# A fused cross-attention and gated feed-forward kernel: Q projected straight into transposed form, rotated over partition halves, and weights loaded in place

## The reference

```python
q = (layernorm(x) @ Wq).reshape(b, t, 32, 128)          # 32 query heads
k = (ctx @ Wk).reshape(b, t, 8, 128); v = (ctx @ Wv).reshape(b, t, 8, 128)
q, k = rope(q), rope(k)                                  # x*cos + rotate_half(x)*sin
logits = 30 * tanh(q.k * 0.0884 / 30)                    # 4 query heads share one k, v
w = softmax(where(mask, logits, -1e30))
x = x + tanh(g_xattn) * ((w @ v).reshape(b, t, 4096) @ Wo)
h = layernorm(x)
gate, up = h @ Wg, h @ Wu                                # 512 -> 1376, 4-bit weights
x = x + tanh(g_ffn) * float16((gate * sigmoid(gate) * up) @ Wd)
```

## Time and profile before

| | |
|---|---|
| median of 3 runs | 811.78 us (811.74 to 812.43) |
| the profiled execution | 811.05 us, span 809.3 us, mean granted clock 0.982 |
| busy in the span | PE 772.4, PEld 644.7, DVE 616.4, ACT 352.7, POOL 494.1 us |
| instructions | 12403 |

### The profile page before, as it was taken

The page is one execution under the profiler, slowest core; times in us unless marked ns, Lnnn a source line. Parts: engine busy times, 40 slices in busy tenths (PEclk is TensorE's granted clock), DMA queues, the critical chain, the costliest instruction groups (busy, mean ns, idle before and its releaser), DMA issues.

```text
span 809.3 us, 12403 instructions
## 1 busy us (share of the span) xinstructions
PE 772.4 (95%) x3905; PEld 644.7 (80%) x3905; DVE 616.4 (76%) x1290; ACT 352.7 (44%) x715; POOL 494.1 (61%) x391
## 2 busy tenths in 40 slices
PE   4799999999999999999999999999998689999998
PEld 3677888888888888888888888888876468888786
DVE  6798887788878887788878887786897587787531
ACT  3545443444345443444444443444443345555520
POOL 3689766566656666566665666567885466666400
PEclk9989999999999999999999999999999799999999
DMA  8410402010210201020111102020010134342011
GB/s 294 130 53 1 131 1 79 1 53 0 80 52 1 79 1 53 1 79 1 53 38 41 53 2 62 18 47 1 21 42 1 42 72 114 98 107 49 0 66 39
DMA packets 56995, 41.61 MB, mean 51 GB/s; under 512 B 22922, under 2 KB 44298, under 8 KB 56938
## 3 DMA queue, kind: packets, MB, share of 16 engines
q1 hardware_dynamic: 56938, 40.90, 17.3%
HBM read 38.77 MB, written 2.11 MB: 51 GB/s over the span
## 4 chain that ended last, share of the span: by engine, by line
PE 89%; DVE 6%; POOL 3%; issue 2%; ACT 1%; DMA 0%; DVEq 0%; ACTq 0%; POOLq 0%
PE ps_o L53 7%; PE ps_o L55 7%; PE ps_o L54 7%; PE bank_q L55 7%; PE bank_q L53 7%; PE bank_q L54 7%; PE ps_qT L1131 4%; PE bank_kv L54 3%; PE bank_kv L55 3%; PE bank_kv L53 3%; PE ps_pv L53 3%; PE ps_s L54 3%; PE ps_s L53 3%; PE ps_s L55 3%; PE ps_pv L54 2%; PE ps_pv L55 2%
## 5 line engine op out<-in xcount | busy, mean ns | idle before, releaser
L511 POOL TENSOR_TENSOR aT_lo<-attn,aT_hi 128x512 fp32r<-128x512 f32 x64 | 96.8, 1512 | 157.8 <-ACT aT_hi L679 157.8
L53 PE MATMUL bank_q<-wq_hi,xT_hi 128*128 128x512 f32 x256 | 108.4, 424 | 1.6 <-DVE wq_lo L807 1.6
L638 ACT CAST qT_hi<-ps_qT 128x512 fp32r<-128x512 f32 x64 | 37.5, 586 | 162.1 <-PE bank_kv L1132 88.7
L55 PE MATMUL bank_q<-wq_hi,xT_lo 128*128 128x512 f32 x256 | 102.8, 401 | 0.0
L54 PE MATMUL bank_q<-wq_lo,xT_hi 128*128 128x512 f32 x256 | 102.7, 401 | 0.0
L53 PE MATMUL ps_o<-wo_hi,aT_hi 128*128 128x512 f32 x256 | 101.0, 394 | 1.2 <-POOL acc L490 0.7
L54 PE MATMUL ps_o<-wo_lo,aT_hi 128*128 128x512 f32 x256 | 100.1, 391 | 0.0
L55 PE MATMUL ps_o<-wo_hi,aT_lo 128*128 128x512 f32 x256 | 100.1, 391 | 0.0
L524 POOL TENSOR_TENSOR roped<-q_cos,q_sin 128x512 f32<-128x512 f32 x61 | 79.1, 1296 | 12.2 <-DVE q_sin L833 12.2
L496 POOL TENSOR_TENSOR probs<-probs,keepT 128x512 f32<-128x512 f32 x64 | 83.7, 1308 | 3.0 <-ACT probs L655 2.9
L988 DVE SCALAR_TENSOR_TENSOR acc<-ps_o,tgates,acc 128x512 f32<-128x512 f32 x54 | 40.5, 751 | 54.5 <-PE ps_o L55 54.5
(11 more groups left out here) (220 smaller groups left out, 2218.1 us busy)
## 6 DMA issues: line engine op xcount, KB each, us to landing
wo_raw<-in_Wo SPq DMA_DIRECT2D x8, 1024.0 KB, 5.3
wq_raw<-in_Wq SPq DMA_DIRECT2D x7, 1024.0 KB, 5.8
packed<-in_gate_q SPq DMA_DIRECT2D x40, 64.0 KB, 2.2
packed<-in_up_q SPq DMA_DIRECT2D x40, 64.0 KB, 2.3
packed<-in_down_q SPq DMA_DIRECT2D x10, 256.0 KB, 3.3
acc<-in_x SPq DMA_DIRECT2D x8, 256.0 KB, 8.4
cT_raw<-in_ctx SPq DMA_DIRECT2D x8, 256.0 KB, 8.5
wkv_raw<-in_Wk SPq DMA_DIRECT2D x8, 256.0 KB, 5.9
```

Of the source, the lines that this page charges most:

```text
L53: nc.tensor.matmul(out, w_hi, m_hi, start=first, stop=False)
L55: return nc.tensor.matmul(out, w_lo, m_hi, start=False, stop=last)
L511: nc.gpsimd.tensor_tensor(aT_lo[:], attn[:], aT_hi[:].bitcast(F32), ALU.subtract).then_inc(a_split, 1)
L638: nc.scalar.copy(qT_hi[:], ps_qT[:])
```

## The change

- **Q is made transposed.** Job n makes, for one head and four sequences, the tile of 128 head columns by 512 tokens: 128 columns of Wq are at rest and the four sequences of x move (`make_q`). It writes to two banks in turn. Eight jobs make a group, in the order half, head; job s+4 runs in slot s, and the first four ahead of slot 0, for which four sequences must be ready (eight for job 4). Slots 60 to 63 have no job.
- **Q's transposes are gone**; K's stays (`transpose_k`).
- **The rotation** now lies across partitions. VectorE makes the cosine product over 128 partitions and the sine products over the partition halves, 64 by 512 each, reading one half of the bank and writing the other half of `q_sin` (`cos_q`). GpSimd adds into `q_rot`, an SBUF tile for both halves of the sequences. ScalarE and VectorE split Q from `q_rot`, not from a PSUM bank. A transposed table of cosine and sine comes in as another input, and rows of the mask's table are turned on TensorE once.
- **Weights in place.** The raw weights land where their `lo` part will stand, so that there are two raw buffers; a load waits for the projections that used the tile two groups before (q_done, kv_done, o_done). Wk and Wv are split in two parts of two blocks each (128x512), no longer in four of 128x256.
- **The start**: x of all sequences is normalised, turned and split ahead of slot 0, with VectorE subtracting for x and GpSimd for the first weights. The context follows beside slots 0 to 5.
- **No loop** over slots: all 67 are straight code. Some tiles of the feed-forward part lie elsewhere.

TensorE at a slot's start, before: four Q transposes, K's, then the old projection (the numbers tell the buffers apart).

```diff
-        wq_raw = sb("wq_raw", [P, KT, GC], F32)
...
+        def split_pair(name, shape, starts, hi, lo, raw):
+            starts.append(at[0])
+            par = len(hi)
+            hi.append(sb(f"{name}_hi{par}", shape, F32R))
+            raw.append(over(f"{name}_raw{par}", shape, F32, at[0]))
+            lo.append(sb(f"{name}_lo{par}", shape, F32R))
...
+        q_rot = sb("q_rot", [P, 2, HG, HALF, T], F32)
+        k_rot = sb("k_rot", [P, D], F32)
...
+        q_banks = [bank[:].rearrange("p (b t) -> p b t", b=HALF) for bank in (bank_q, bank_q2)]
...
+        def q_job(n):
+            return n // B, n % B // HALF, n % HALF
         def all_slots(eng, slot):
...
+            for s in range(SLOTS + 3):
+                slot(s)
...
+                def load_wq(g):
+                    wait(sp, q_done, (g - 1) * B)
+                    sp.dma_start(wq_raw[g % 2][:], wq_v[:, :, g * GC:(g + 1) * GC]).then_inc(ld_wq[g % 2], 16)
...
+                def rope(n):
+                    g, half, h = q_job(n)
+                    pool.wait_ge(q_mul, n + 1)
+                    wait(pool, qk_split, n - h - AHEAD)
+                    nc.gpsimd.tensor_tensor(q_rot[:, half, h, :, :], q_cos[:], q_sin[:], ALU.add).then_inc(q_roped, 1)
...
-                    wait(act, tr_done, j + 1)
-                    wait(act, s_done, j)
-                    nc.scalar.copy(qT_hi[:], ps_qT[:])
...
+                def round_q(s):
+                    act.wait_ge(q_roped, (s // HALF + 1) * HALF)
+                    wait(act, s_done, s)
+                    nc.scalar.copy(qT_hi[:], q_rot[:, s % B // HALF, :, s % HALF, :]).then_inc(q_rounded, 1)
...
+                def cos_q(n):
+                    dve.wait_ge(q_done, n + 1)
+                    wait(dve, q_roped, n)
+                    h = D // 2
+                    nc.vector.tensor_tensor(q_cos[:], q_banks[n % 2], q_tab[:, 0, :].unsqueeze(1).to_broadcast([P, HALF, T]),
+                                            ALU.mult)
+                    nc.vector.tensor_tensor(q_sin[0:h], q_banks[n % 2][h:D], q_tab[h:D, 1, :].unsqueeze(1).to_broadcast([h, HALF, T]),
+                                            ALU.mult)
+                    nc.vector.tensor_tensor(q_sin[h:D], q_banks[n % 2][0:h], q_tab[0:h, 1, :].unsqueeze(1).to_broadcast([h, HALF, T]),
+                                            ALU.mult).then_inc(q_mul, 1)
...
-                    nc.vector.tensor_tensor(qT_lo[:], ps_qT[:], qT_hi[:].bitcast(F32), ALU.subtract)
+                    dve.wait_ge(q_rounded, s + 1)
+                    nc.vector.tensor_tensor(qT_lo[:], q_rot[:, s % B // HALF, :, s % HALF, :], qT_hi[:].bitcast(F32), ALU.subtract)
+                    dve.wait_ge(k_rounded, s + 1)
...
-                    for h in range(HG):
-                        nc.tensor.transpose(ps_qT[:, h * T:(h + 1) * T], roped[:, h, :], ident[:])
-                    nc.tensor.transpose(kv_bank(s)[:, 2, :], roped[:, HG, :], ident[:]).then_inc(tr_done, 1)
...
+                def make_q(n):
+                    g, half, h = q_job(n)
+                    par, seqs, cols = g % 2, slice(half * HALF, (half + 1) * HALF), slice(h * D, (h + 1) * D)
...
+                    if n % HALF == 0 and g == 0:
+                        pe.wait_ge(x_lo, (half + 1) * HALF)
+                    wait(pe, q_mul, n - 1)
+                    for k in range(KT):
...
+                        mm = split_matmul(nc, q_banks[n % 2], wq_hi[par][:, k, cols], wq_lo[par][:, k, cols],
+                                          xT_hi[:, seqs, k, :], xT_lo[:, seqs, k, :], k == 0, k == KT - 1)
+                    mm.then_inc(q_done, 1)
...
+                for n in range(AHEAD):
+                    make_q(n)
+                    prep(AHEAD + n)
...
                 def slot(s):
                     if runs(s - 1) and s != SLOTS:
+                        transpose_k(s - 1)
+                    if 0 < s and has_q_job(s):
+                        make_q(s + AHEAD)
                     if runs(s):
+                        make_kv(s)
```

More of the change, by code:

```diff
@@ L223, in flamingo_block @@
         ld_tab, ld_mask, ld_gates = sem("ld_tab"), sem("ld_mask"), sem("ld_gates")
-        ld_wq, ld_wkv, ld_wo = sem("ld_wq"), sem("ld_wkv"), sem("ld_wo")
+        ld_wq, ld_wkv, ld_wo = ([sem(f"ld_{w}{par}") for par in range(2)] for w in ("wq", "wkv", "wo"))
         id_zero, id_done, half_done = sem("id_zero"), sem("id_done"), sem("half_done")
@@ L270, in steps, with parts_of, has_q_job @@
                 step(0, n)
-        early_parts = [[], [(0, 4), (0, 5)], [(0, 6), (0, 7)], [(1, 0), (1, 1)], [(1, 2)], [(1, 3), (1, 4)],
-                       [(1, 5), (1, 6)], [(1, 7)]]
-        def all_slots(eng, slot):
-            for s in range(B):
-                slot(0, 0, s)
-            for s in range(B, SLOTS - B):
-                base = (s - B) // LOOPED * LOOPED
-                slot(base, base // B, s - base)
-            for s in range(SLOTS - B, SLOTS + 3):
-                slot(0, 0, s)
+        early_parts = [[("wo", 0, 0), ("wo", 0, 1), ("wq", 1, 0)], [("wo", 0, 2), ("wo", 0, 3), ("wq", 1, 1)],
+                       [("wq", 1, 2), ("wq", 1, 3), ("wkv", 1, 0)], [("wkv", 1, 1)]]
+        def parts_of(s):
+            if 0 <= s < HALF:
+                return early_parts[s]
+            g, b = s // B + 1, s % B
+            parts = [("wq", g, b + 2) if b < 2 else ("wkv", g, b - 2) if b < HALF else ("wo", g, b - HALF)]
+            if b >= B - 2:
+                parts.append(("wq", g + 1, b - B + 2))
+            return [part for part in parts if s >= 0 and part[1] < KV]
+        def has_q_job(s):
+            return s + AHEAD < SLOTS
+        def q_job(n):
+            return n // B, n % B // HALF, n % HALF
+        def all_slots(eng, slot):
+            for s in range(SLOTS + 3):
+                slot(s)
         def runs(s):
@@ L350, in _ @@
                              zero_bytes[0:ZERO_ROWS_DOWN, 2, :]).then_inc(zero_stored, 16)
-                load_wo(1)
-                with sp.Fori(2, KV) as g:
-                    load_wqkv(g)
+                for g in range(2, KV):
+                    load_wq(g)
+                    load_wkv(g)
                     load_wo(g)
@@ L452, in invert_std2 @@
+                split_w("wq", 0, 2)
+                split_w("wq", 0, 3)
+                invert_std(4)
+                split_w("wkv", 0, 0)
+                invert_std(5)
+                split_w("wkv", 0, 1)
+                ctx_rest(0)
+                invert_std(6)
+                rope(0)
+                invert_std(7)
+                ctx_rest(1)
+                for n in range(1, AHEAD):
+                    rope(n)
                 def invert_std2(b):
@@ L497, in apply_mask, with slot @@
                                             ALU.mult).then_inc(masked, 1)
-                def slot(base, group, s):
-                    j = base + s
+                def slot(s):
                     if s == SLOTS:
@@ L514, in slot @@
                         add_share(s)
-                    if s == 0:
-                        prep(1)
-                    if s + 2 < B:
-                        prep(s + 2)
-                    if s >= B and runs(s + B):
-                        split_w(group + s // B + 1, s % B, (s // B + 1) % 2)
-                    if s >= DVE_ADDS and runs(s):
-                        wait(pool, q_mul, j + 1)
-                        wait(pool, tr_done, j)
-                        nc.gpsimd.tensor_tensor(roped[:, 0:HG, :], q_cos[:], q_sin[:], ALU.add).then_inc(q_roped, 1)
-                    if s == 1:
-                        pool.wait_ge(tab_done, 1)
+                    if has_q_job(s):
+                        rope(s + AHEAD)
                     if runs(s - 1) and s != SLOTS:
-                        apply_mask(j - 1, s - 1)
+                        apply_mask(s - 1)
                     if s == SLOTS:
                         p_rest(s + 1)
-                    if s + 3 < B:
-                        invert_std(s + 3)
-                    if s < B:
-                        for head, part in early_parts[s]:
-                            split_w(head, part, head)
                     if s >= TAIL + 4:
@@ new lines, in make_kv @@
+                def make_kv(s):
+                    g, b = s // B, s % B
+                    if s < B:
+                        pe.wait_ge(ctx_lo[b], 1)
+                    if b == 0:
+                        pe.wait_ge(wkv_split, (g + 1) * 2)
+                    wait(pe, qk_split, s - 1)
+                    if s == TAIL + AHEAD + 1:
+                        pe.wait_ge(q_mul, SLOTS)
+                    for k in range(KT):
+                        mm = split_matmul(nc, kv_bank(s)[:, 0:2, :].rearrange("p h d -> p (h d)"),
+                                          cT_hi[:, b, k, :], cT_lo[:, b, k, :],
+                                          wkv_hi[g % 2][:, k, :], wkv_lo[g % 2][:, k, :], k == 0, k == KT - 1)
+                    mm.then_inc(kv_done, 1)
```

548 lines of the change are left out of this document (267 added, 281 removed).

## The result

The changed kernel takes **858.9 us** (median of 4 runs, 854.94 to 859.35), the kernel before on the same chip 811.76 (810.87 to 812.43). The ratio is 1.057, 95% interval 1.054 to 1.060. The forecast was 799.7, range 790 to 809: it is wrong, and on the other side of no change. The profiled execution took 854.94 us with a span of 852.8, the fastest of the four, so what follows explains 43.5 us of span, and the median is 4 us worse.

A forecast was written before the change was run, and what follows sets the result against it. PE was taken to bound the kernel by setting the middle slot. 811.05 (profiled) − 22.9 (transposes) + 1.5 (lock) + 11.8 (start) − 2.5 (tail) = 798.95; with the median 0.73 higher, 799.7 us, range 790 to 809.

The forecast's parts named there:

- The projection and its transposes: PE's middle slots: new projection form costs 0, Q's transposes go, 0.44 us a slot, 9.118 to 8.68; 22.9 us off.
- Does VectorE keep up: Middle slot: sine halves add 0.54 us, VectorE's slot becomes 8.0 (7.5 to 8.1), below PE's 8.68, so PE still sets it.
- my 7.46: VectorE's working time in a middle slot before the change: 9.12 less 1.66 us of waits.
- The lock: Middle slots: VectorE and POOL exclude each other on SBUF; qT_lo held in two slots of eight; 1.5 us added.
- My 1.5 us: Added over the middle for slots where holding by POOL still reaches PE; bounds 0 and 11.
- The rival with a whole POOL instruction lost: Middle: VectorE loses 1.3 us to POOL each slot, 8.0 + 1.3 = 9.3; total 833 us; chance 0.08.
- The Trainium skill: Its SBUF section: two-SBUF-input VectorE ops and SBUF-reading POOL ops take turns for whole instructions; said to speak against the edit.
- The start: Up to slot 8: more VectorE work ahead of slot 1 (near 47 us), slot 8 at 107.4 against 95.62; 11.8 us on.
- The tail: Slots 60 to 63, which have no job: 37.6 us against 40.1 before; 2.5 us off (0 to 6).
- Loads and unrolling: Weights loaded in place and loops made straight code: cost 0, nothing gained; 2 to 3 us per group if Wo's copy waits.

The follow-up runs named there:

- first reordering: The changed kernel with POOL's weight part moved behind aT_lo instead of ahead of it: 835.05 us, ratio 1.029.
- the two orders without one: Changed kernel with POOL's aT_lo and weight parts behind p_lo, 812.19 us; first reordering with ACT's weight rounding ahead of aT_hi, 814.94 us.
- POOL in order: The changed kernel with POOL waiting for p_lo's signal, then doing aT_lo, then the weight parts: 812.19 us, ratio 1.001.
- Spare matmuls: 12 matmuls of 512 columns, result unread, added in each of slots 60 to 63 to the kernel with POOL in order: 806.4 us, ratio 0.994.
- the order on ACT: Kernel with POOL in order, and ACT rounding Q ahead of scaling the share in slots 57 to 64: 802.75 us, ratio 0.990.

## Why the prediction was wrong, point by point

- **The projection and its transposes: right.** With nothing in its way the slot is 8.69 (forecast 8.68), over slots 4 to 59, and the moving operand in four pieces costs nothing.
- **Does VectorE keep up: mis-sized, and nearly right.** Freed, DVE's slot is 8.69 − 0.45, less the 0.08 by which acc starts earlier behind attn when it needn't wait (0.61 after attn's start, not 0.69): 8.16, against 8.0 with bounds up to 8.1. The sine halves cost more than I gave them: the three products take 2.12 us where the earlier trace rows had 1.26, so 0.86 and not 0.54. The 0.16 that this doesn't explain is the same 0.08 twice, for the two waits inside my 7.46. The rows of 96 partitions told rightly that fewer partitions don't help. They begin at partition 0 and so couldn't tell the 0.1 that each change of the first partition adds.
- **The lock: this step failed.** I had read the mechanism (the two exclude each other for a whole instruction) and did the clock work for it: mask to 7.9, weight part to 0.47 into the next slot, qT_lo at 0.79. In the freed kernel (aT_lo and weights behind p_lo) the slot whose rows are shown opens at 302.06; its mask ends at 310.39, 8.33 into it, and 0.32 of the 0.43 that I was short are the sine products. A weight part behind it would end 0.90 into the next slot, and qT_lo wants to start at 302.92 − 302.06 = 0.86. So it is held, by little. That alone would make 8.16 + 0.44 = 8.60, still below PE's 8.69. The hold that costs is the other, aT_lo ahead of p_lo, and I never timed those two against each other. The first reordering has it without any hold of qT_lo: 8.16 + 0.93 = 9.09, measured 9.07. In the freed kernel ScalarE has aT_hi ready at 303.67, and POOL follows 0.08 later in the first reordering (315.60, 315.68), so aT_lo could start at 303.75 where p_lo starts at 303.72: a tie, which in that reordering falls to aT_lo by 0.23.

```profile
303.05 0.62 ACT L712 CAST aT_hi<-attn 128x512 fp32r<-128x512 f32 x1
```

  With both holds it is 8.16 + 0.44 + 0.90 = 9.50, and DVE stops waiting for PE. From there the distances are DVE's own: from q_sin's end to qT_lo's start it needs 3.3 us (304.71 to 308.03), POOL's rotation, mask and weight part need 3.8 (304.79 to 308.60), and they overlap in each slot. My 1.5 us were for holds in two slots of eight; they are in every slot, and the measured price is 48 × (9.48 − 8.69) = 38 us. How the slots come to the held state is worked out from the freed trace and not shown; that the length goes when the overlap goes is shown by the two orders without one (812.19 and 814.94 us). The rival with a whole POOL instruction lost (DVE slot 9.3, 833 us) was this case, with a chance of 0.08: right in mechanism, 0.2 us short in the slot, and with too small a share for the ends.
- **The Trainium skill.** SBUF — State Buffer, section "SBUF: two separate sides", says that whichever of the two starts first has the ports for the whole instruction and the other blocks. The traces agree in every pair shown (aT_lo at 315.68, p_lo at 315.91 taking 1.61). I wrote that it spoke against the edit and then gave its outcome 0.08.
- **The start: half right.** Slot 1 at 47.06 (forecast 47). Slot 8 at 117.06, not 107.4. With POOL in order it is 110.9: 6.2 of the 9.7 were the lock again, in slots 3 to 7 (52.5 us, then 45.1, though slot 1 starts 1.2 later), which I had priced at 9.5 and four times 8.8. The other 3.5 are 1.3 at slot 1 and 2.6 in slots 1 to 3 (9.34, 8.19 and 10.31 against 8, 7.7 and 9.5), less 0.4 in slots 4 to 7.
- **The tail: wrong in sign.** I gave 37.6 us at full clock, up to the end of slot 63's output projection, against 40.1 before; it takes 46.3. Two things were missing. Work taken from PE at the place where nothing else fills it lets the granted clock fall. The windows to the last transpose, in the kernel before and in the changed one:

```profile
569.60:606.47 36.87, 35.49 (x198) 29.97 (x196) 32.50 (x75) 18.36 (x38) 31.50 (x26) 1.00 0.14 34
```
```profile
606.75:648.72 41.97, 29.30 (x134) 23.30 (x132) 32.81 (x67) 17.48 (x37) 30.50 (x24) 0.83 0.12 30
```

  PE is busy for 35.5 of 36.9 us at full clock before, and for 29.3 of 42.0 at 0.83 now, so that the remaining matmuls last longer (wo's are 0.43 us apart at 594 us of the first reordering, 0.23 in the middle). And Q, ready four slots ahead, is rounded behind the share all the same. Spare matmuls and the order on ACT each take 7 to 9 us back.
- **Loads and unrolling: right** to 0.3 us behind slot 63's output projection; between 300 and 450 us nothing waits for a DMA.
